# SyncE's order of loads, store and weights in the attention steps of a gated cross-attention and expert kernel

## The reference

```
x = x + tanh(g_xattn) * attention(layernorm(x), ctx, mask)   # scores over 375 context rows, softmax, readout
x = x + tanh(g_ffn)   * experts(layernorm(x), Wg, W, b)      # top-1 of 8 experts, each 512 x 512
```

## Time and profile before

| quantity | value |
|---|---|
| median of 3 runs | 386.59 us (382.66 to 387.85) |
| the profiled execution's own time | 384.22 us |
| its span, first to last instruction | 382.2 us |
| TensorE matmul busy | 355.3 us, 93% |
| VectorE busy | 301.6 us, 79% |
| ScalarE busy | 222.5 us, 58% |
| GpSimd busy | 227.1 us, 59% |
| mean granted TensorE clock | 0.989 of full speed |
| DMA traffic | 67.65 MB, mean 177 GB/s |

### The profile page before, as it was taken

One profiled execution on the slowest core, in us unless ns is written; L12 is line 12 of the kernel. 1 busy time (PEld: TensorE's weight loads), 2 busy tenths in 40 slices (PEclk: granted clock), 3 DMA queues, 4 the chain that ended last, 5 costly groups with the idle time before them and its releaser, 6 DMA issues.

```text
span 382.2 us, 9646 instructions
## 1 busy us (share of the span) xinstructions
PE 355.3 (93%) x2052; PEld 299.8 (78%) x2053; DVE 301.6 (79%) x1087; ACT 222.5 (58%) x520; POOL 227.1 (59%) x482
## 2 busy tenths in 40 slices
PE   6799999999999999999999899797999999999980
PEld 6688888888888888888878688675777888888760
DVE  4668898898898898998989989868777676777660
ACT  3577777777777777767767667623433444444410
POOL 5144766666666667566556566747666566667530
PEclk9999999999999999999999999999999999999995
DMA  8948788778979877989876776854545444444400
GB/s 217 269 130 229 195 194 239 193 195 225 211 190 212 219 186 199 238 178 210 230 184 165 189 184 166 266 130 112 165 140 159 145 149 147 133 151 145 158 31 0
DMA packets 31442, 67.65 MB, mean 177 GB/s; under 512 B 10578, under 2 KB 11094, under 8 KB 31416
## 3 DMA queue, kind: packets, MB, share of 16 engines
q1 hardware_dynamic: 24600, 50.74, 52.2%
q0 software_dynamic: 6624, 16.58, 14.0%
q10 hardware_dynamic: 192, 0.03, 0.1%
HBM read 52.06 MB, written 17.10 MB: 181 GB/s over the span
## 4 chain that ended last, share of the span: by engine, by line
PE 57%; DMA 11%; issue 9%; DVE 8%; POOL 8%; ACT 2%; SPq 1%; POOLq 1%; DVEq 1%; ACTq 0%
PE read_both L1194 10%; PE ctx_ps L1135 9%; PE read_both L1195 9%; DMA ctx_sb<-in_ctx 5%; POOL out_rows L606 5%; DMA x_sb<-mid_rows,take 5%; PE score_ps L1160 4%; PE score_ps L1157 4%; PE score_ps L1158 4%; PE score_ps L1159 4%; PE prob_ps L1144 3%; POOL x_sb L597 2%; PE score_ps L1229 2%; PE score_ps L1231 2%; PE score_ps L1230 2%
## 5 line engine op out<-in xcount | busy, mean ns | idle before, releaser
L1194 PE MATMUL read_both<-ctx_sb,turned 125*112 125x264 f32 x192 | 61.1, 400 | 2.2 <-issue 1.8
L987 DVE TENSOR_TENSOR ctxT_lo<-ctx_ps,ctxT_hi 128x375 fp32r<-128x375 f32 x96 | 49.3, 541 | 13.1 <-ACT ctxT_hi L636 12.9
L1229 PE MATMUL score_ps<-w_hi,ctxT_hi 128*128 x140 | 58.4, 417 | 0.0
L530 POOL DMA_INDIRECT token_list<-pay,pos x32 | 32.2, 1008 | 42.3 <-DVE pos L907 41.0
L1195 PE MATMUL read_both<-ctx_sb,turned 125*112 125x256 f32 x192 | 57.1, 379 | 0.0
L1135 PE MATMUL ctx_ps<-ident,ctx_sb 125*128 125x125 f32 x384 | 52.3, 271 | 4.6 <-DMA ctx_sb<-in_ctx 3.0
L1231 PE MATMUL score_ps<-w_lo,ctxT_hi 128*128 x140 | 55.3, 395 | 0.0
L1230 PE MATMUL score_ps<-w_hi,ctxT_lo 128*128 x140 | 55.1, 393 | 0.0
L597 POOL DMA_INDIRECT x_sb<-mid_rows,take x35 | 34.9, 996 | 29.6 <-DVE ctx_sb L947 15.3
L606 POOL DMA_INDIRECT out_rows<-ctx_sb,put x35 | 39.6, 1130 | 17.1 <-issue 9.2
L645 ACT ACTIVATE rn<-x_sb,li 128x512 f32<-128x512 f32 x35 | 28.5, 815 | 33.7 <-DMA x_sb<-mid_rows,take 33.7
(11 more groups left out here) (142 smaller groups left out, 815.5 us busy)
## 6 DMA issues: line engine op xcount, KB each, us to landing
ctx_sb<-in_ctx SPq DMA_DIRECT2D x32, 682.5 KB
w_raw<-in_L_ffn_W SPq DMA_DIRECT2D x32, 256.0 KB, 4.6
x_sb<-in_x SPq DMA_DIRECT2D x32, 224.0 KB, 3.9
mid_rows<-x SPq DMA_DIRECT2D x32, 224.0 KB, 2.8
ctx_sb<-in_ctx SPq DMA_DIRECT2D x32, 79.2 KB
ctx_sb<-in_L_ffn_b SPq DMA_DIRECT2D x8, 256.0 KB
li<-token_list SPq DMA_DIRECT2D x35, 2.0 KB, 2.0
x_sb<-mid_rows,take POOLq DMA_INDIRECT x35, 3.5
```

The lines of the kernel that those rows point to most:

```text
L987: dve.tensor_tensor(ctxT_lo[:, k, 0:M], ctx_ps[k % 2][:, 0:M], ctxT_hi[:, k, 0:M].bitcast(F32), ALU.subtract).then_inc(ctxT_ok, 1)
L1194: pe.matmul(read_a, weight, values[:, 0:E + HALF], start=(c == 0), stop=(c == MC - 1))
L1229: pe.matmul(y_ps[a][:, :], hi, w_hi[:, chunk], start=(k == 0), stop=False)
```

## The change

In SyncE's step the three loads of four batches ahead are issued first, then the store of x2, then the weights. A wait for x2 of batch i stands ahead of all of them. The waits inside `keep` and `next_w` are as they were.

```diff
             def batch(i):
+                sp.wait_ge(x2_ok, i.times(1, 1))
+                load(i.plus(4))
+                keep(i)
                 next_w(i)
-                keep(i)
-                load(i.plus(4))
```

## The result

The changed kernel takes 445.1 us in the median of 4 runs (440.0 to 447.2), the kernel before 387.2 us (382.7 to 388.5). The forecast was 425 us with a range of 402 to 440. The direction and the mechanism were right, the size was not: the change cost 56 to 58 us where 40.5 were worked out.

The account below looks back on a forecast made before the run. TensorE bounds the kernel at 7.23 us a step; late weights close a two-step loop of 2.26 + 6.20 + 0.59 + 7.57 + 1.03 = 17.65 us, adding 40.5 us over 28 steps to 384.2: 424.7, say 425, range 402 to 440.

Parts of the forecast that it names:

- The bound before: Attention stage of the kernel before: TensorE, busy 93% of the span, sets an undisturbed step at 7.23 us.
- Loads and store: SyncE's step: loads issued 0.53 us earlier give back at most 3.0 us; the store behind them costs nothing.
- The weights' issue: SyncE's step: weights of piece i+2 are issued 2.26 us after x2(i), 5.6 us later than before.
- Their landing: DMA queue: weights land 6.2 us after issue, behind x, context and store; own range 5.4 to 7.2 us.
- The loop: Attention stage: x2, weights, fourth context part, scores, TensorE's step, x2 take 17.65 us for two steps, 8.8 a step.
- Its consumer: ScalarE waits for the weights ahead of the fourth context part, so they must land about 5.3 us after x2(i).
- so I leave the clock as it is: TensorE in attention steps: busy 82%, clock stays at 2.4 GHz, as in an expert-stage stretch busy 80%.
- 1.6 us in each step: TensorE ahead of its scores in the attention stage: idle 1.6 us in every step, waiting for ScalarE's context part.
- (d): TensorE's clock falls to 1.2 GHz in the pauses: up to 101 us on top of the forecast; chance 0.02.
- (a): Queue does not hold the weights back: landing 4.6 us, 8.03 us a step, +18.2 us, 402 us; chance 0.12.
- (b): Weights land within 3.0 us, so the loop does not bind; earlier context loads give 381 us; chance 0.06.
- (c): DMA bursts collide: weights land after 8.1 to 8.9 us, +67 to +78 us, 451 to 463 us; chance 0.05.

## Why the prediction was wrong

*The bound before* was read rightly: 0.8 us more TensorE work a step cost 24 us.

*Loads and store* were sized rightly: nothing measurable, 0.998 (0.994 to 1.003). The store behind the loads cost nothing.

*The weights' issue*, 2.26 us after x2, came at 2.2 to 2.4 in the middle of the stage (1.7 in seven steps near its ends). *Their landing*, taken as 6.2 us, has a median of 6.2. The addends were less right than the sum: I gave 1.6 us to the bytes of store and weights, and the kernels without them gained at most 0.4 us in the landing. That 6.2 came out is in part luck.

*The loop*, 17.65 us for two steps, was named and sized rightly but for one term, TensorE's step of 7.57 us. The turn shown above takes 168.30 - 148.90 = 19.40 us; TensorE's step in it, from its first score matmul at 148.90 to the end of its last readout at 157.93, took 9.03 us and not 7.57, and all other terms together are 0.3 us over the sum. Its consumer was named rightly: moving ScalarE's wait took 40 us off.

**The failed step is "so I leave the clock as it is".** It went by the mean of the earlier trace rows, where TensorE was busy for 80% and the clock stayed, against 82% forecast. A mean does not show the length of one pause. The stretch of rows 10 holds one pause, of 2.03 us, and ends 0.9 us before that pause does; the loop made ten of 1.9 to 4.4 us, one in every second step, because it fixes the sum of two steps and not each. Assuming "1.6 us in each step" was part of the same step. And rows 10 were a single case: in the kernel with the weights ahead of the wait for x2, the pause in the same place of the expert stage was 1.95 us, and 3.4 us at the half clock followed it.

The cost can be read directly. The steps of TensorE that followed the eight pauses of 2.4 us and more took 8.8 to 10.3 us each, from the first score matmul to the end of the last readout, where the steps at full clock take 7.5 to 7.6 (one took 8.5); that is 14.2 us in all, and the loop runs through each of these steps. It agrees with the 28 steps, 261.4 us instead of 247.0, 14.4 more. Filling the pauses took 9 to 13 us off the whole kernel, by medians or by ratios; in part that may be the sooner landing (5.7 to 6.1 us instead of 6.2), which the runs do not separate. And the mean clocks, 0.948 of 437.9 us and 0.989 of 382.2 us, give 2 x 0.052 x 437.9 = 46 and 2 x 0.011 x 382.2 = 8 us at the half clock, 37 us more, which can cost up to half of that, 19 us.

The rival for it, (d), had a chance of 0.02 and a price of up to 101 us. Both were off: the clock did fall, in part of the steps, for 14 us. The rule of the Trainium skill that the prediction set against rows 10 ("TensorE: Matmul & The Clock Gate", "HAM oscillation — how this bites in real kernels") was the better guide; the trace agrees with it in part, with 0.50 granted after 0.30 us of work in 2.60, but only at 8 of the 18 pauses ahead of the scores and not at each.

*Rivals (a), (b) and (c)* did not come about: the landing was neither 4.6 us nor 8.1. Of the signs named, ScalarE's wait (22 times, 2.6 us each), the landing near 6 us and the weights' issue 2.1 us after the first load came; the clock near 0.99, the 247 us and TensorE's even idle time of 1.6 us a step did not. At 440.0 us, the fastest run lies on the upper end of the range.

What stays open is why single landings vary from 5 to 7 us, and which pauses let the clock fall. The length of the pause alone does not decide: in the kernel with the 8 KB weights, pauses of 2.98, 2.87 and 2.67 us (ending at 92.3, 109.9 and 127.3 us) left it at 1.00, and the 1.95 us above was followed by the half clock. How often it falls in a given run probably makes the 7 us between the runs of the changed kernel; their clocks go from 0.948 at 440.0 us to 0.933 at 447.2.

## What to carry to other kernels

Here a DMA at the end of a burst landed late with all that was issued just ahead of it, though it was small. So issue last what has the longest time until its use, and look for the wait that the late one gates: here it stood ahead of work that did not need it. Where a delay closes a loop over several steps, work out the longest single pause of TensorE and not its mean idle time; if the pauses gather in one step, the clock can fall and add its own cost.

## What the runs showed of the hardware

Idle time of TensorE can cost more than itself: with the pauses filled by 16 small matmuls a step, the kernel got 10 to 13 us faster, and 24 cost no more than 16. In the changed kernel's trace the half clock came at each of the eight pauses of 2.4 us and more and at none of the ten shorter ones; other runs have exceptions both ways (2.98 us without it, 1.95 us with it). A DMA of 8 KB behind 986 KB of loads and a store of 224 KB landed 5.8 us after its issue, and one of 256 KB 6.2 us, on one queue; ahead of them, 256 KB took 4.4 us. Moving a store of 224 KB from ahead of a load to behind it changed that load's time to landing by 0.1 us.
